# Mixture of experts: the first layer with stationary weights, each tile's weights brought by a DMA of its own

## What is computed

```python
xm = _ln(x, ln2_g, ln2_b).reshape(B * S, D)          # 2624 tokens, D = 192
logits = xm @ router_w.T + router_b
probs = jax.nn.softmax(logits, axis=-1)
topw, topi = jax.lax.top_k(probs, K)                 # K = 2 of E = 8 experts
topw = topw / jnp.sum(topw, axis=-1, keepdims=True)
combine = jnp.zeros((T, E), xm.dtype).at[jnp.arange(T)[:, None], topi].add(topw)
out = jnp.zeros_like(xm)
for e in range(E):
    h = jax.nn.gelu(xm @ w1[e] + b1[e], approximate=False)   # 192 -> 768
    y = h @ w2[e] + b2[e]                                    # 768 -> 192
    out = out + combine[:, e:e + 1] * y
x = x + out.reshape(B, S, D)
```

## Time and profile before

| | us |
|---|---|
| median of 3 runs | 1385.61 (1384.7 to 1394.42) |
| the profiled execution, first to last instruction | 1385.7 |
| TensorE busy | 1219.3 |
| VectorE busy | 1016.9 |
| POOL busy | 745.5 |
| ScalarE busy | 690.1 |

### The profile page before, as it was taken

The page is one execution under the profiler, slowest core; times in us unless marked ns, Lnnn a source line. Parts: engine busy times, 40 slices in busy tenths (PEclk is TensorE's granted clock), DMA queues, the critical chain, the costliest instruction groups (busy, mean ns, idle before and its releaser), DMA issues.

```text
span 1385.7 us, 19455 instructions
## 1 busy us (share of the span) xinstructions
PE 1219.3 (88%) x5828; PEld 782.3 (56%) x5829; DVE 1016.9 (73%) x1934; ACT 690.1 (50%) x1467; POOL 745.5 (54%) x469
## 2 busy tenths in 40 slices
PE   7996767477998989898987789999999999999996
PEld 4342334133454545454552458888888677777774
DVE  5899696998998989999999745788879653333332
ACT  1147431776767676777756235555543332222221
POOL 3037670877888786969697320135545564222222
PEclk9798868798999999999999999999999699999998
DMA  6200001440404040322320001112222132222221
GB/s 183 58 1 0 31 9 47 169 147 1 146 0 147 1 145 27 120 63 83 108 71 1 0 9 58 42 49 73 59 62 82 39 63 46 36 37 37 35 35 21
DMA packets 72799, 81.17 MB, mean 59 GB/s; under 512 B 13282, under 2 KB 64705, under 8 KB 72721
## 3 DMA queue, kind: packets, MB, share of 16 engines
q1 hardware_dynamic: 53386, 69.29, 16.0%
q0 software_dynamic: 17152, 9.24, 5.0%
q10 hardware_dynamic: 2184, 1.72, 0.5%
HBM read 48.87 MB, written 30.01 MB: 57 GB/s over the span
## 4 chain that ended last, share of the span: by engine, by line
PE 59%; DVE 20%; ACT 10%; issue 6%; POOL 2%; DMA 1%; DVEq 0%; SPq 0%; ACTq 0%; POOLq 0%
PE ps L2239 10%; PE ps L2258 6%; PE ps L1021 6%; DVE hs L1305 6%; PE ps L1623 3%; PE ps L1681 3%; PE ps L932 3%; PE ps L257 3%; PE ps L250 3%; PE ps L1696 2%; ACT ps L1174 2%; PE ps L2248 2%; PE ps L998 2%; PE ps L957 2%; ACT prod L378 2%
## 5 line engine op out<-in xcount | busy, mean ns | idle before, releaser
L1423 POOL TENSOR_TENSOR Bx<-dtz,Bb 128x984 f32<-128x984 f32 x128 | 289.5, 2281 | 45.0 <-DVE hs L1305 31.2
L1305 DVE TENSOR_TENSOR_SCAN hs<-ps,Bx 128x492 f32<-128x492 f32 x256 | 287.7, 1165 | 22.1 <-POOL Bx L1423 12.8
L1174 ACT ACTIVATE ps<-dt,A 128x324 f32<-128x324 f32 (+1 forms) x512 | 211.5, 456 | 79.5 <-DVE hs L1305 77.3
L1021 PE MATMUL ps<-hs,b_id 128*128 128x492 f32 x512 | 238.5, 588 | 12.0 <-DVE y L1272 9.3
L2358 POOL DMA_INDIRECT out<-yt,dest x48 | 74.7, 1556 | 170.8 <-DVE yt L2344 158.2
L1315 DVE TENSOR_TENSOR hs<-hs,ps 128x984 f32<-128x984 f32 x128 | 150.3, 1174 | 2.5 <-issue 0.5
L2239 PE MATMUL ps<-W,xT 97*128 (+1 forms) x384 | 143.7, 518 | 3.1 <-issue 2.0
L1021 PEld LDWEIGHTS ps<-hs,b_id 128*128 128x128 f32 x512 | 92.9, 195 | 79.7 <-issue 74.3
L2328 DVE COPY hT__5717<-ps 128x768 f32<-128x768 f32 x48 | 46.0, 958 | 112.1 <-PE ps L2248 110.7
L2296 ACT ACTIVATE hb<-ps 128x768 f32<-128x768 f32 x48 | 38.9, 811 | 143.3 <-PE ps L2239 143.3
L2258 PE MATMUL ps<-W,hT__5717 128*128 x576 | 109.3, 327 | 0.8 <-DVE yb L2338 0.8
(11 more groups left out here) (277 smaller groups left out, 2402.2 us busy)
## 6 DMA issues: line engine op xcount, KB each, us to landing
Bb<-b_rows SPq DMA_DIRECT2D x32, 656.0 KB, 7.1
buckets<-b_zero SPq DMA_DIRECT2D x8, 2288.0 KB, 15.4
xg<-buckets SPq DMA_DIRECT2D x48, 104.0 KB, 2.0
xc<-in_xcol SPq DMA_DIRECT2D x4, 1176.0 KB, 9.6
W<-in_w1d SPq DMA_DIRECT2D x8, 582.0 KB
W<-in_w2d SPq DMA_DIRECT2D x8, 576.0 KB
out<-H SPq DMA_DIRECT2D x8, 246.0 KB
H<-P SPq DMA_DIRECT2D x8, 147.0 KB
```

Source lines behind the costliest of these rows:

```text
L1021: mm = pe.matmul(ps[:, BANK_Y + h, 0:HALF], ident[:], f2(hs[:, s % LONG])[:, h * HALF:(h + 1) * HALF], start=s == 0, stop=s == STATE - 1)
L1174: a = act.activation(ps[:, BANK_A + h, c:c + w].rearrange("p (g t) -> p g t", t=S)[:, :, 1:S], dt[:, (par + t // STATE) % 2, m, g0 * S:g1 ...
L1305: v.tensor_tensor_scan(f2(hs[:, t % LONG])[:, c], ps[:, BANK_A + h, 0:HALF], f2(Bx[:, t % RING])[:, c], 0.0, ALU.mult, ALU.add).then_inc(s ...
L1423: g.tensor_tensor(Bx[:, t % RING], dtz[:, p], Bb[:, p, t % STATE, :].rearrange("p (a n) -> p a n", a=1).broadcast_to([128, NI, N]), ALU.mu ...
```

## The change

The first layer is turned round. A tile's weights are now stationary, in six slices of 128 units, and its tokens (`xT`) move, 128 columns each time; the result has the units of the middle layer on partitions, which is what the second layer needs. So `flip`, `hb` and VectorE's copy are gone, gelu writes `hT` itself, and the middle layer of odd and even tiles has banks of its own (`hidden_bank`). A step of TensorE is now `turn` of tile j+2, `up` of tile j+1, `down` of tile j. `W1` no longer holds all experts but four slots (`W_SLOTS`): SP reads `te[j]` and loads the weights of that tile's expert into slot j % 4, 97 partitions with 6,144 bytes each, after the `xg` load of the same tile and under the same waits. The first four are issued as soon as the table is there, ahead of `xg` 0 and 1. `w1d` in DRAM has the expert ahead of the two halves, so that a row of 6,144 bytes is contiguous.

```diff
@@ sync
             for e in range(EXPERTS):
-                sp.dma_start(W1[:, :, e, :], w1d[:, :, e, :]).then_inc(s_e, 16)
                 sp.dma_start(W2[:, :, e, :], w2d[:, :, e, :]).then_inc(s_e, 16)
...
             sp.wait_ge(s_tab, 1)
+            for j in range(W_SLOTS):
+                t.weights(j, j)
             sp.wait_ge(s_sc, FULL_ROUNDS * (16 * 2 * G))
             t.load(0, 0)
             t.load(1, 1)
...
             for j in range(4, FIRST):
                 t.again(j, j % 2)
+                t.weights(j, j % 4)
@@ tensor, the steps between the last attention round
             step(i, par, 0)
-            pe.wait_ge(s_e, 32 * EXPERTS)
+            pe.wait_ge(s_e, 16 * EXPERTS)
             pe.wait_ge(s_tab, 1)
             pe.wait_ge(s_E, ROUNDS * G)
-            t.up(0, 0, t.expert(0))
-            pe.wait_ge(ex.s_xT, 2)
+            t.up(0, 0)
             step(i, par, 1)
             route(i, par, 1)
-            t.up(1, 1, t.expert(1))
+            pe.wait_ge(s_PTa, ROUNDS * G)
+            t.turn(2, 0)
+            t.up(1, 1)
             step(i, par, 2)
@@ experts, loads
+            def weights(j, p4):
+                e = sp.value_load(te[0:1, bass.ds(j, 1)] if not isinstance(j, int) else te[0:1, j:j + 1],
+                                  min_val=0, max_val=EXPERTS - 1)
+                sp.dma_start(W1[:, p4].rearrange("p (a k) n -> p a (k n)", a=1),
+                             w1d[:, bass.ds(e, 1), :, :].rearrange("p a k n -> p a (k n)")).then_inc(s_W[p4], 16)
@@ experts, tensor
-            def up(j, p, e):
-
+            def up(j, p4):
+
+                p = p4 % 2
                 pe.wait_ge(s_xT, j + 1)
+                pe.wait_ge(s_W[p4], per_weights(j, p4))
                 if isinstance(j, int) and j == 0:
                     pe.wait_ge(s_cst, 1)
-                at_least(pe, s_ge, j)
-                for h in range(2):
+                at_least(pe, s_ge, j if isinstance(j, int) and j < 3 else j - 1)
+                for m in range(KF):
                     for k in range(2):
                         c_ = slice(0, HD + k)
-                        mm = pe.matmul(ps[:, UP + h, 0:384], xT[c_, p, k, :],
-                                       W1[c_, k, bass.ds(e, 1), h * 384:(h + 1) * 384].rearrange("p a n -> p (a n)"),
-                                       start=k == 0, stop=k == 1)
+                        mm = pe.matmul(ps[:, hidden_bank(j, p) + m // 3, m % 3 * 128:(m % 3 + 1) * 128],
+                                       W1[c_, p4, k, m * 128:(m + 1) * 128], xT[c_, p, k, :], start=k == 0, stop=k == 1)
                 mm.then_inc(s_h, 1)
 
-            def flip(j, p):
-                pe.wait_ge(s_ge, j + 1)
-                at_least(pe, s_hT, j)
-                for k in range(KF):
-                    mm = pe.transpose(ps[:, FLIPPED + k // 3, (k % 3) * 128:(k % 3 + 1) * 128], hb[:, p, k * 128:(k + 1) * 128], ident[:])
-                mm.then_inc(s_ht, 1)
...
+            def lead(j, p):
+                if is_tile(j + 2):
+                    turn(j + 2, p % 2)
+                if is_tile(j + 1):
+                    up(j + 1, (p + 1) % 4)
+
             def step(j, p4):
...
+                lead(j, p4)
                 if is_tile(j):
...
+                    down(j, p4 % 2)
@@ experts, scalar
             def hidden(j, p):
                 act.wait_ge(s_h, j + 1)
-                act.activation(hb[:, p, :].rearrange("p (a n) -> p a n", a=2), ps[:, UP:UP + 2, 0:384], ACT.Gelu).then_inc(s_ge, 1)
+                if not isinstance(j, int) or j >= 2:
+                    act.wait_ge(s_y, j - 1)
+                bank = hidden_bank(j, p)
+                act.activation(hT[:, p].rearrange("p (a k) n -> p a (k n)", a=2), ps[:, bank:bank + 2, 0:384], ACT.Gelu).then_inc(s_ge, 1)
@@ layout and places
-    w1 = np.zeros((97, 2, 8, 768), f32)
+    w1 = np.zeros((97, 8, 2, 768), f32)
...
-    w_experts, end = stack(top, ("W1", 2 * EXPERTS * DFF * F), ("W2", KF * EXPERTS * D * F))
+    w_experts, end = stack(top, ("W1", W_SLOTS * 2 * DFF * F), ("W2", KF * EXPERTS * D * F))
```

More of the change, by code:

```diff
@@ L625 @@
 KF = DFF // 128
+W_SLOTS = 4
 U32 = mybir.dt.uint32
@@ L1519, in attention @@
         s_b2 = sem("e_b2")
-        ex = experts(nc, ctx, at, ps, out, W1, W2, te, to, ident, vec, xs, s_s, s_tab, s_b2)
+        ex = experts(nc, ctx, at, ps, out, W1, W2, te, to, ident, vec, xs, w1d, s_b2)
         FRONT, NEWS = 1, -2
@@ L1804, in _ @@
             step(i, par, 1)
+            t.affine(2, 0)
             step(i, par, 2)
             t.hidden(1, 1)
-            t.affine(2, 0)
             gate_exp(ROUNDS - 2)
@@ L2063, in _ @@
             rank(ROUNDS - 2)
-            t.step(0, 0)
             normed(ROUNDS - 1, 1 - par)
@@ L2071, in _ @@
             place(ROUNDS - 2)
-            t.step(2, 2)
+            t.step(1, 1)
             pick(ROUNDS - 1)
             rank(ROUNDS - 1)
-            t.step(3, 3)
+            t.step(2, 2)
             offsets(ROUNDS - 1)
@@ L2079, in _ @@
             other_tiles()
+            t.step(3, 3)
+            which_experts(FIRST, TILES + 1 - FIRST, le_rest)
             t.step(4, 0)
-            which_experts(FIRST, TILES + 1 - FIRST, le_rest)
-            t.step(5, 1)
             which_rows(FIRST, TILES + 1 - FIRST, le_rest, fl[:, 0:1])
-            for j in range(6, FIRST):
+            for j in range(5, FIRST):
                 t.step(j, j % 4)
@@ L2148, in _, with experts @@
             t.done()
-def experts(nc, ctx, at, ps, out, W1, W2, te, to, ident, vec, xs, s_s, s_tab, s_b2):
+def experts(nc, ctx, at, ps, out, W1, W2, te, to, ident, vec, xs, w1d, s_b2):
     if True:
@@ L2159, in sem @@
             return ctx.enter_context(nc.semaphore(name))
-        xg = sb("xg", [128, 2, RW]); xT = sb("xT", [HD + 1, 2, 2, 128]); hb = sb("hb", [128, 2, DFF])
+        xg = sb("xg", [128, 2, RW]); xT = sb("xT", [HD + 1, 2, 2, 128])
         hT = sb("hT_", [128, 2, KF, 128]); yb = sb("yb", [128, 2, D]); yt = sb("yt", [128, 4, D]); b2 = sb("b2", [128, EXPERTS, D])
         tail = sb("tail", [128, 4, EXPERTS + 1]); dest = sb("dest", [128, 4], U32)
-        UP, FLIPPED, Y = 0, 3, 5
+        Y = 5
         s_xg = [sem("e_xg0"), sem("e_xg1")]
+        s_W = [sem(f"e_W{p}") for p in range(W_SLOTS)]
         s_cst = sem("e_cst"); s_tx = sem("e_tx"); s_xT = sem("e_xT"); s_h = sem("e_h"); s_ge = sem("e_ge"); s_cp = sem("e_cp")
-        s_ht = sem("e_ht"); s_hT = sem("e_hT"); s_y = sem("e_y"); s_yb = sem("e_yb"); s_yt = sem("e_yt"); s_add = sem("e_add")
+        s_y = sem("e_y"); s_yb = sem("e_yb"); s_yt = sem("e_yt"); s_add = sem("e_add")
         ex = Stage()
@@ L2173, in turned, with hidden_bank @@
             return {0: 7, 1: 6}.get(j, 2) if isinstance(j, int) else 2
+        def hidden_bank(j, p):
+            return 0 if p == 0 or (isinstance(j, int) and j == 1) else 3
         def rest_of(engine, step, first):
@@ L2190, in per_slot, with per_weights @@
             return (j // 2 + 1) * 16 if isinstance(j, int) else (j - p) * 8 + 16
+        def per_weights(j, p4):
+            return (j // 4 + 1) * 16 if isinstance(j, int) else (j - p4) * 4 + 16
         def loads(sp):
@@ L2203, in again @@
                 load(j, p)
+            def weights(j, p4):
[3 more added lines that the diff above has]
+                             w1d[:, bass.ds(e, 1), :, :].rearrange("p a k n -> p a (k n)")).then_inc(s_W[p4], 16)
             def rest():
-                for j in (FIRST, FIRST + 1):
+                for j in range(FIRST, FIRST + 4):
                     again(j, j % 2)
[L2208 to L2212, removed]
+                    weights(j, j % 4)
+                with sp.Fori(FIRST // 4 + 1, TILES // 4) as i:
+                    for p4 in range(4):
+                        again(i * 4 + p4, p4 % 2)
+                        weights(i * 4 + p4, p4)
+            t.load, t.again, t.weights, t.rest = load, again, weights, rest
             return t
@@ L2323, in step @@
             def step(j, p4):
-                p = p4 % 2
-                e_out = expert(j - 1) if is_tile(j - 1) else None
-                if is_tile(j):
-                    v.wait_ge(s_ht, j + 1)
-                    v.tensor_copy(hT[:, p].rearrange("p (a k) n -> p a (k n)", a=2), ps[:, FLIPPED:FLIPPED + 2, 0:384]).then_inc(s_hT, 1)
                 if is_tile(j + 2):
```

70 lines of the change are left out of this document (28 added, 42 removed).

## The result

The changed kernel takes 2252.12 us (median of 4 runs, 2243.3 to 2253.06), against 1385.15 us (1384.13 to 1394.42) for the kernel before in the same session. The ratio is 1.6262, with a 95% interval from 1.6193 to 1.6331: 63% slower. The forecast was 2310 us, 2235 to 2380. The profiled execution took 2251.25 us, its span 2249.4 us.

What follows compares the result with a forecast made beforehand. TensorE bounded the kernel before; after the change, one DMA engine carrying each tile's weights would. Load 4 begins at 1196.5 us, plus 44 loads 1084.6, 16 scatters 5.5 and an end of 23.3: 2310 us, range 2235 to 2380.

Steps and rivals of the forecast that it cites:

- The forecast's likeliest case: Expert tiles: one DMA engine kept busy by the weight loads sets the pace, 2310 us; chance 0.88.
- A load of 97 partitions runs on one engine: First layer's weight load: 97 gives one of 16 engines, at 25.6 GB/s, 23.3 us per load.
- The start: Before the tile loop: first load at 1057 us, first turn near 1154 us, load 4 begins at 1196.5 us.
- The rate: Engine time per tile: load 23.3 us, plus xg 0.38 and POOL's adds 0.98, about 24.7 us; 44 loads make 1084.6 us.
- The bound from below: Weight load: 0.227 us per packet of 6,144 bytes, worked out from two packet sizes, gives 22.0 us per load.
- Scatters: POOL's scatters on the loads' engine: 0.35 us each, 16 of them after load 4 begins add 5.5 us.
- The end: From the last weights' landing to the end: first layer, two second layers, VectorE, POOL's chain and finish, 23.3 us.
- Where TensorE waits: Each tile's first layer: TensorE waits for the DMA of W, some 19 us; xg lands some 24 us or more after issue.
- The compute: TensorE per tile: first layer of 24 passes 2.64 us, flips gone; tile 4.98 us in place of 5.68, 0.70 less.
- rival A: Weight load spreads over the engines, 2 us, hidden inside TensorE's 4.98 us per tile: 1355 us; chance 0.05.
- B: Weight loads use one engine each, but another each time, three side by side: 8.2 us per tile, 1518 us; chance 0.02.
- C: Only one weight load outstanding, so each tile adds 2 us landing and TensorE's 9 us: 2794 us; chance 0.04.

Runs made afterwards that it cites:

- e1_rows98: Changed kernel with a 98th row of zeros, which nothing reads, added to the first layer's weights and slots; 1356.66 us, ratio 0.9767 to the kernel before.
- e2_rows106: Changed kernel with the first layer's weights padded to 106 rows (2 x 53) in place of 97; 1753.37 us (one run).
- e5_start97: Changed kernel, 97 rows, only SP's order changed: at the start xg goes ahead of its tile's weights, output copies in between; 2216.54 us (one run).
- e9_halves: Changed kernel, 97 rows, each tile's weights brought by two DMAs with packets of 3,072 bytes in place of one with 6,144; 2271.19 us (one run).
- e8_adds2: Changed kernel, 97 rows, POOL's accumulating DMA adds only the first 2 of a tile's 128 rows; 2221.95 us (one run).
- e4_first4: Changed kernel with 98 rows and the loads of tiles 4 to 47 left out, reusing the first four tiles' weights; 1345.64 us, ratio 0.9748 to before.

## Why the prediction was right, and where its sum was off

The forecast's likeliest case came true, and the time lies 58 us, 2.5%, below the forecast, within its range. The sum was made for the span, and that lies 60.6 us below (2249.4): 55.4 by the rate of the loads, 2.6 by the start, 0.9 by the scatters and 1.6 by the end, all in the same direction.

1. **A load of 97 partitions runs on one engine: right.** The share of 7.7%, the single packet under way, `e1_rows98` and `e2_rows106` show it.
2. **The start: right.** First load at 1057 us forecast, 1056.4 measured; four loads done at 1153, measured 1150.8; first turn 1154.5, measured 1151.73; load 4 begins at 1196.5, measured 1193.9. `e5_start97` shows what was behind it, as told there.
3. **The rate: the mis-sized term.** The step "the load 23.3 + 0.38 + 0.98 = 24.65 us" is 23.39 measured (982.3 us over 42 loads, from load 6 on). 44 times the 1.26 us of difference is 55.4 us. The greater part of it is the load itself: 22.4 and not 23.3 us, 0.9 too much. The figure came from a row with packets half as long, rounded to two digits and over a stretch of 12 us. `e9_halves` gives 0.4 to 0.5 us to the length of the packets, so the rest is the rounding and the short stretch. The bound from below, 22.0 us at 0.227 us per packet, was worked out from two sizes and was the better guess. The other part is POOL's adds: "0.98 us" was their whole share of the engine, and `e8_adds2` measured 0.41 to 0.47, 0.5 too much. The two together are 1.4 us, more than the 1.26: with 22.4, 0.38 for `xg` and 0.41 to 0.47 a load would be 23.2 to 23.3 us, and 0.1 to 0.2 us of the 23.39 remain that neither the sum nor a run names.
4. **Scatters: about right.** Loads 4 and 5 took 26.3 and 24.2 us beside the last scatters and the later ones 23.0 to 23.7. The 44 loads took 1033.8 us in all, 4.6 us more than 44 x 23.39, where 5.5 were forecast.
5. **The end: right.** From the last weights (about 2227.7 us) to the end of the span it is 21.7 us, 23.3 forecast. The last first layer took 5.46 us (5.1 forecast), the second layers less than forecast (2.69 and 2.21 us against 3.9), since the clock had risen.
6. **Where TensorE waits: wrong.** "TensorE waits for the DMA of W at each first layer" isn't what the rows show. It waits at the turning, for `xg`, since the turning of tile j+2 stands ahead of the first layer of tile j+1 on TensorE, and `xg` j+2 stands behind weights j+1 on the engine; by the time it has landed, these weights have too. The wait is 15 to 17 us, not 19, and the landing 39.8 us ("24 or more"). It changes no time: it is the same queue, seen at another of its doors. A reader who goes by the name in the wait alone would take the 104 KB of `xg` for the cause.
7. **The compute: right where it could be seen.** Twelve matmuls of 128 columns take 2.68 us from start to start (1246.16 to 1248.84) in `e1_rows98`, just what 8 passes of 384 took before; a tile is 4.85 us, 4.98 forecast. At 98 rows the gain of 24 us by the medians stands against 44 x 0.70 = 30.8 in rival A's sum, and `e4_first4` bounds what the loads may still cost.
8. **Rivals.** B (another engine each time) and C (the queue runs dry) have no trace in the rows: from 1193.9 us on the loads follow each other one at a time, with at most 0.6 us between two. The estimate of 3.4 us beside rival A comes from a formula for GpSimd's DMAs, and these are SP's; with 98 rows a load's packets took 2.8 us from the first to the last (median, 1200 to 1300 us).

## What to carry to other kernels

Before a transfer is moved into a loop, look at what share of the 16 engines it had when it ran once: 6.4% is a sixteenth, and a load that nobody waited for can be the bound once it comes per tile. A bias row that makes 97 out of 96 is a case to look for; a row of padding, or a DMA of its own for the odd row, mends it. When a wait names a small transfer that lands late, ask what stands ahead of it in its queue, and time a queue by the distance between its packets, not by how long one takes or by its mean share.

## What the runs showed of the hardware

- 97 rows, 98 rows: 2252.12 and 1356.66 us. The row count alone makes some 895 us. Packets of 6,144 bytes under way at once, most often: 1 with 97 rows, 2 with 106, 14 with 98, 16 with 96.
- The packets of the accumulating DMA cost the load that shares an engine with them only about half of their own time there (0.41 to 0.47 of 0.98 us per tile, `e8_adds2`).
- TensorE's 24 passes of 128 columns take the time of 8 passes of 384 (2.68 us each), although they load the stationary side three times as often: at the full clock (1.00 in this stretch) those loads cost no time beside passes of 128 columns.
- How much SP's queue takes before its issues block seems to go by packets and not by bytes. Four loads of 97 packets kept SP for 54.84 us, the same bytes as eight DMAs of 97 packets for 75.70 us (both rows stand above), so fewer bytes were queued when the last was issued; and in the loop `xg` landed 22.3 us after its issue in place of 39.9 (medians from 1300 to 2200 us). No run was made to settle it.
